# Six-layer kernel on one core: the RWKV layer's reciprocal as exp(-ln x), its norms and last product on other engines

## What is computed

```python
x = _layernorm(x, ln_g, ln_b)
last_x = jnp.pad(x[:, :-1], ((0, 0), (1, 0), (0, 0)))
k = (x * time_mix_k + last_x * (1.0 - time_mix_k)) @ Wk.T     # v and r likewise
td = jnp.exp(time_decay)
def step(carry, kv):                                          # over the tokens
    num, den = carry; kt, vt = kv                             # kt = exp(k)
    den = den * td + kt
    num = num * td + kt * vt
    return ((num, den), num / (den + 1e-08))
out = jax.nn.sigmoid(r) * wkv @ Wo.T
```

## Time and profile before

| | us |
|---|---|
| median of 3 runs | 2185.0 |
| lowest, highest | 2184.05, 2187.51 |
| profiled execution, its own time | 2186.31 |
| span of that execution | 2184.6 |
| TensorE busy in the span | 1656.4 (76%) |
| VectorE busy | 1514.8 (69%) |
| ScalarE busy | 965.0 (44%) |
| GpSimd busy | 1043.2 (48%) |

### The profile page before, as it was taken

How to read it: one execution, slowest core, us unless ns; L and a number is a source line. 1 busy time by engine, 2 the same in 40 slices (tenths; PEclk the granted TensorE clock), 3 DMA queues, 4 the chain that set the end, 5 groups by cost and what they waited for, 6 DMA issues and landing times.

```text
span 2184.6 us, 43737 instructions
## 1 busy us (share of the span) xinstructions
PE 1656.4 (76%) x11008; PEld 1493.4 (68%) x11008; DVE 1514.8 (69%) x4465; ACT 965.0 (44%) x2292; POOL 1043.2 (48%) x1639
## 2 busy tenths in 40 slices
PE   6499999378838999985168996269999974199993
PEld 6399999366627999984157776268888863177772
DVE  6678888288876888886546665758888865366664
ACT  2476665022207666632035554036666621055551
POOL 3537675378832455324633333605666625533331
PEclk9999999599969999985589998559999965599996
DMA  3110000720001001020111111202111101111115
GB/s 154 35 35 31 30 30 2 186 52 0 0 7 54 31 25 29 16 80 31 39 50 50 51 39 43 58 22 69 58 58 56 49 1 41 51 47 51 47 35 159
DMA packets 95511, 103.82 MB, mean 48 GB/s; under 512 B 12328, under 2 KB 75965, under 8 KB 94880
## 3 DMA queue, kind: packets, MB, share of 16 engines
q1 hardware_dynamic: 62144, 72.42, 10.7%
q10 hardware_dynamic: 23328, 12.67, 2.5%
q0 software_dynamic: 9920, 17.35, 2.4%
HBM read 67.94 MB, written 37.97 MB: 48 GB/s over the span
## 4 chain that ended last, share of the span: by engine, by line
PE 40%; DVE 30%; issue 14%; ACT 5%; another core or an unknown queue 2%; POOL 2%; DMA 2%; DVEq 2%; ACTq 1%; SPq 1%; POOLq 0%
PE banks L533 5%; ACT top_hhi L592 3%; PE banks L1037 3%; DVE bnstats L238 3%; DVE rwkv_over L1516 3%; PE banks L522 2%; PE banks L1024 2%; PE banks L1039 2%; PE banks L1038 2%; PE banks L1026 2%; PE banks L1025 2%; DVE top_hlo L752 2%; PE banks L1060 2%; PE banks L1059 2%
## 5 line engine op out<-in xcount | busy, mean ns | idle before, releaser
L803 POOL DMA_INDIRECT rt_y<-top_y,top_xs x182 | 178.8, 982 | 331.4 <-DVE top_y L760 307.8
L1235 DVE TENSOR_TENSOR choice_hlo<-choice_h,choice_hhi 128x512 fp32r<-128x512 f32 x256 | 180.1, 744 | 89.7 <-ACT choice_hhi L1122 89.5
L1114 ACT ACTIVATE choice_h<-banks 128x512 f32<-128x512 f32 x256 | 152.4, 599 | 160.7 <-PE banks L1026 142.5
L752 DVE TENSOR_TENSOR top_hlo<-banks,top_hhi 128x384 fp32r<-128x384 f32 x182 | 101.4, 557 | 144.6 <-ACT top_hhi L592 130.4
L796 POOL DMA_INDIRECT rt_rows<-top_payload,top_slot x128 | 129.7, 1013 | 131.2 <-DVE top_slot L713 94.0
L533 PE MATMUL banks<-t_w,top_hhi 128*128 x364 | 131.0, 360 | 45.9 <-DVE top_hlo L752 23.1
L746 DVE SCALAR_TENSOR_TENSOR top_h<-top_silu,top_xs,banks 128x176 f32<-128x176 f32 x364 | 128.4, 394 | 45.7 <-ACT top_silu L587 43.6
L1037 PE MATMUL banks<-choice_hhi,ec_w_hi 128*128 128x256 f32 x512 | 147.6, 288 | 4.2 <-DVE choice_hlo L1235 3.5
L1024 PE MATMUL banks<-choice_xin_hi,ec_w_hi 128*128 128x256 f32 x512 | 147.2, 287 | 4.7 <-ACT choice_xin_lo L1107 4.7
L1122 ACT ACTIVATE choice_hhi<-choice_h 128x512 fp32r<-128x512 f32 x256 | 146.4, 624 | 0.0
L1026 PE MATMUL banks<-choice_xin_hi,ec_w_lo 128*128 128x256 f32 x512 | 143.8, 281 | 0.0
(11 more groups left out here) (305 smaller groups left out, 5835.5 us busy)
## 6 DMA issues: line engine op xcount, KB each, us to landing
choice_token_row<-choice_tokens SPq DMA_DIRECT2D x64, 256.0 KB, 3.1
mlstm_run_row<-mlstm_run SPq DMA_DIRECT2D x32, 512.0 KB, 3.6
rt_rows<-rt_blank ACTq DMA_DIRECT2D x2, 6188.0 KB, 35.4
top_xs<-rt_rows SPq DMA_DIRECT2D x182, 68.0 KB
top_y_in<-rt_y SPq DMA_DIRECT2D x16, 512.0 KB, 7.2
X<-in_x SPq DMA_DIRECT2D x8, 512.0 KB, 6.8
ec_stage<-in_ec_w SPq DMA_DIRECT2D x2, 2048.0 KB, 15.6
out_x<-X SPq DMA_DIRECT2D x8, 512.0 KB, 7.6
```

Source lines behind the costliest of these rows:

```text
L803: pool.indirect_dma_start(d.y[self.run], bass.IndirectOffsetOnAxis(ap=at, axis=0), self.y[:, u % self.YR, :], None, bounds_check=NT * P - ...
L1114: act.activation(self.h[:, c, :], self.ph[c][:, :], ACT.Gelu).then_inc(self.gelu_done, 1)
L1235: dve.tensor_tensor(flat(self.hlo), self.h[:, c, :], flat(self.hhi).bitcast(F32), ALU.subtract).then_inc(self.hlo_done, 1)
```

## The change

What it does, in the RWKV layer:

- VectorE's reciprocal is replaced. ScalarE makes log = ln(under) and guess = exp(-log); VectorE makes off = under * guess and over = (off - 2) * guess, one Newton step, which gives minus the reciprocal; the sign is taken back by a negated copy of Wo, made once. er1 is capped at 1e18.
- The product z = num * over goes from VectorE to GpSimd.
- This layer's norm and the next layer's norm go from GpSimd (two passes) to ScalarE, as Identity with a scale and a bias per partition, one instruction for each 128 tokens. The bias, -mean/std, is one more small GpSimd product per sequence, in this layer's and in the layer before's scale step.
- Output and update of a sequence come one step later, and the statistics, scale, next layer's transposes, copies and scores too; there is one more step in the pipeline. The loop is entered after eight steps in place of six. Next layer's norm stays at its place (s-4 on ScalarE, where it was s-3 on GpSimd).

```diff
@@ Moments
-            self.chains.append(Chain(steps, self.PER[kind == "rwkv"], base))
+            per = 7 if kind == "rwkv" else 2 if self.by_scalar(n) else 1
+            self.chains.append(Chain(steps, per, base))
...
+        def product(ins):
+            ch.link(pool, ins)
+            return pool.tensor_tensor(flat(self.nmrs), flat(self.nm), flat(self.rs), ALU.mult)
@@ Normed
+    def scalar(self, act, b, u, xn_free):
+        m = self.sh.moments
+        act.wait_ge(m.scaled, self.layer * B + b - self.o + 1)
+        xn_free()
+        for t in range(TP):
+            scale, bias = (v[:, bass.ds(b - self.o, 1), t:t + 1].rearrange("p a t -> p (a t)") for v in (m.rs, m.nmrs))
+            i = act.activation(self.xn[:, u, t, :], self.sh.X[:, bass.ds(TP * (b - self.o) + t, 1), :].rearrange("p a c -> p (a c)"),
+                               ACT.Identity, scale=scale, bias=bias)
+        i.then_inc(self.done, 1)
@@ Rwkv.tensor
-            if self.next is not None and inside(b - 6):
-                pe.wait_ge(self.next.xT_done, self.next.o + b - 5)
+            if self.next is not None and inside(b - 7):
+                pe.wait_ge(self.next.xT_done, self.next.o + b - 6)
...
-            if inside(s - 1):
-                out(s - 1, 1 - u)
+            if inside(s - 2):
+                out(s - 2, u)
...
-                if inside(s + 1) and inside(s - 4):
+                if inside(s + 1) and inside(s - 5):
                     pe.wait_ge(self.x1_done, s + 2)
-                self.ahead_for_next(pe, self.next.turn_first, s - 4, u)
-                self.ahead_for_next(pe, self.next.score, s - 5, 1 - u)
+                self.ahead_for_next(pe, self.next.turn_first, s - 5, 1 - u)
+                self.ahead_for_next(pe, self.next.score, s - 6, u)
@@ Rwkv.scalar
+        def guess(b, u):
+
+            act.wait_ge(self.under_done, b + 1)
+            need(act, self.over_done, 2 * (b - 1))
+            act.activation(self.log[:, u, :], self.under[:, u, :], ACT.Ln).then_inc(self.guess_done, 1)
+            act.wait_ge(self.guess_done, 2 * b + 1)
+            act.activation(self.guess[:, u, :], self.log[:, u, :], ACT.Exp, scale=-1.0).then_inc(self.guess_done, 1)
...
         def step(s, u):
+            if inside(s - 1):
+                guess(s - 1, 1 - u)
             if inside(s + 1):
                 x1(s + 1, 1 - u)
             if inside(s):
                 exps(s, u)
+            if inside(s + 2):
+                norm(s + 2, u)
             if self.next is not None:
-                self.ahead_for_next(act, self.next.first_xT, s - 4, u)
+                self.ahead_for_next(act, self.next.first_norm, s - 4, u)
+                self.ahead_for_next(act, self.next.first_xT, s - 5, 1 - u)
 
         self.sh.start(act, self.x0)
+        norm(0, 0)
+        norm(1, 1)
         act.wait_ge(self.w_in, 32)
@@ Rwkv.vector
-            dve.reciprocal(self.over[:, u, :], self.under[:, u, :]).then_inc(self.over_done, 1)
-            dve.wait_ge(self.over_done, b + 1)
-            need(dve, self.out_done, b - 1)
-            dve.tensor_tensor(self.z[:, u, :], self.num[:, u, :], self.over[:, u, :], ALU.mult).then_inc(self.z_done, 1)
+        def improve(b, u):
+
+            dve.wait_ge(self.guess_done, 2 * b + 2)
+            dve.tensor_tensor(self.off[:, u, :], self.under[:, u, :], self.guess[:, u, :], ALU.mult).then_inc(self.over_done, 1)
+            dve.wait_ge(self.over_done, 2 * b + 1)
+            if not isinstance(b, int) or b >= 2:
+                apart(dve, self.z_done, b - 1, sh.passed)
+            dve.scalar_tensor_tensor(out=self.over[:, u, :], in0=self.off[:, u, :], scalar=-2.0, in1=self.guess[:, u, :],
+                                     op0=ALU.add, op1=ALU.mult).then_inc(self.over_done, 1)
...
         def step(s, u):
-            self.moments_next(dve, s - 2, u)
             if inside(s):
                 mix(s, u)
+            self.moments_next(dve, s - 3, 1 - u)
             if inside(s - 1):
-                update(s - 1, 1 - u)
+                improve(s - 1, 1 - u)
+            if inside(s - 2):
+                update(s - 2, u)
...
+        dve.tensor_scalar(self.wo[:, :], self.w[:, 3, :], -1.0, None, ALU.mult).then_inc(self.setup, 1)
@@ Rwkv.gpsimd
+        def product(b, u):
+
+            apart(pool, self.over_done, 2 * b + 2, self.sh.passed)
+            if not isinstance(b, int) or b >= 2:
+                apart(pool, self.out_done, b - 1, self.sh.passed)
+            pool.tensor_tensor(self.z[:, u, :], self.num[:, u, :], self.over[:, u, :], ALU.mult).then_inc(self.z_done, 1)
 
         def step(s, u):
-            if inside(s + 2):
-                norm(s + 2, u)
             if inside(s):
                 er1(s, u)
-            self.scale_next(pool, s - 2, u)
-            if self.next is not None:
-                self.ahead_for_next(pool, self.next.first_norm, s - 3, 1 - u)
+            self.scale_next(pool, s - 3, 1 - u)
+            if inside(s - 1):
+                product(s - 1, 1 - u)
```

More of the change, by code:

```diff
@@ L42 @@
 ROUND = float(1 << 23)
+FAR = 1.0e18
 FB = 4
@@ L198, in __init__ @@
         self.rs = mem.take("rstd", [P, B, TP])
+        self.nmrs = mem.take("negmean_rstd", [P, B, TP])
         self.stats, self.moments, self.scaled = sh.sem("stats_done"), sh.sem("moments_done"), sh.sem("scaled")
@@ L202, in __init__, with by_scalar @@
         for n, kind in enumerate(LAYERS):
-            self.chains.append(Chain(steps, self.PER[kind == "rwkv"], base))
-            base += (B if n else XC) * self.PER[kind == "rwkv"]
-    PER = (1, 6)
+            per = 7 if kind == "rwkv" else 2 if self.by_scalar(n) else 1
+            self.chains.append(Chain(steps, per, base))
+            base += (B if n else XC) * per
+    def by_scalar(self, layer):
+        return "rwkv" in LAYERS[max(layer - 1, 0):layer + 1]
     def moments_of(self, dve, layer, b, u):
@@ L255, in rstd @@
         ch.link(pool, pool.tensor_scalar(sm[:, 0, :], var, 1.0, EPS_LN, ALU.mult, ALU.add))
-        if ch.per > 1:
+        def product(ins):
+            ch.link(pool, ins)
+            return pool.tensor_tensor(flat(self.nmrs), flat(self.nm), flat(self.rs), ALU.mult)
+        if ch.per > 2:
             ch.link(pool, pool.tensor_tensor(sm[:, 1, :], sm[:, 0, :], half, ALU.pow))
@@ L262, in rstd @@
             ch.link(pool, pool.tensor_tensor(sm[:, 3, :], sm[:, 2, :], half, ALU.pow))
-            i = pool.tensor_tensor(flat(self.rs), sm[:, 1, :], sm[:, 3, :], ALU.mult)
+            i = product(pool.tensor_tensor(flat(self.rs), sm[:, 1, :], sm[:, 3, :], ALU.mult))
         else:
             i = pool.tensor_tensor(flat(self.rs), sm[:, 0, :], half, ALU.pow)
+            if ch.per > 1:
+                i = product(i)
         ch.end()
@@ L960, in pfirst, with first_norm @@
         return self.sh.banks[7][:, T:2 * T] if self.ahead else self.sh.banks[u][:, 0:T]
-    def first_norm(self, pool, b, u):
-        self.norm.gpsimd(pool, b, u, lambda: apart(pool, self.xT_ready, b - 1, self.sh.passed), self.o)
+    def first_norm(self, act, b, u):
+        self.norm.scalar(act, b, u, lambda: need(act, self.xT_ready, b - 1))
     def turn_first(self, pe, b, u):
@@ L1390, in __init__ @@
         self.x1 = f("x1", [P, 2, T + 1])
-        self.ek, self.er, self.er1, self.ekv, self.num, self.den, self.under, self.over, self.z = (
-            f(n, [P, 2, T]) for n in ("ek", "er", "er1", "ekv", "num", "den", "under", "over", "z"))
+        self.ek, self.er, self.er1, self.ekv, self.num, self.den, self.under, self.z = (
+            f(n, [P, 2, T]) for n in ("ek", "er", "er1", "ekv", "num", "den", "under", "z"))
+        self.log, self.guess, self.off, self.over = (f(n, [P, 2, T]) for n in ("log_under", "guess", "guess_off", "over"))
+        self.wo = f("w_out_negative", [P, C])
         bk = sh.banks
@@ L1434, in project @@
             need(pe, self.ekv_done, b - 1)
-            need(pe, self.er_done, b - 1)
+            need(pe, self.exps_done, 2 * (b - 1))
             for n, (o, done) in enumerate(((self.pkv[u][:, 0:T], None), (self.pkv[u][:, T:2 * T], self.kv_done),
@@ L1479, in exps, with norm @@
             need(act, self.scans_done, b - 1)
-            act.activation(self.ek[:, u, :], self.pkv[u][:, 0:T], ACT.Exp).then_inc(self.ek_done, 1)
+            act.activation(self.ek[:, u, :], self.pkv[u][:, 0:T], ACT.Exp).then_inc(self.exps_done, 1)
             act.wait_ge(self.r_done, b + 1)
             need(act, self.er1_done, b - 1)
-            act.activation(self.er[:, u, :], self.pr[u][:, 0:T], ACT.Exp, scale=-1.0).then_inc(self.er_done, 1)
+            act.activation(self.er[:, u, :], self.pr[u][:, 0:T], ACT.Exp, scale=-1.0).then_inc(self.exps_done, 1)
+        def guess(b, u):
[4 more added lines that the diff above has]
+            act.activation(self.guess[:, u, :], self.log[:, u, :], ACT.Exp, scale=-1.0).then_inc(self.guess_done, 1)
+        def norm(b, u):
+            self.norm.scalar(act, b, u, lambda: need(act, self.xT_ready, b - 1))
```

(2 more changed lines are left out.)

24 lines of the change are left out of this document (11 added, 13 removed).

## The result

The changed kernel takes 2212.2 us (median of 4) against 2186.1 before: a ratio of 1.0123, 95% interval 1.011 to 1.0135. Slower, as forecast, by twice as much: +26 us, where the sum said +13.

The account below looks back on a forecast made before the run. The prediction took VectorE to bound the RWKV layer before, and ScalarE with two table loads after: four intervals at 5.3 us and 27 at 6.4 give +12.2, start +1.6, end -0.7, so 2199 us, range 2184 to 2226.

Parts of the forecast that it names:

- the sum: Whole program: RWKV layer +12.2 us, start +1.6, end -0.7, in all +13.1 on 2186.3 us, giving 2199.
- no wait, and both loads are exposed: ScalarE's ln: `under` ready at about 6.3 us, ln not before 7.47, so neither table load hides in a wait.
- the clock's term: TensorE at 1.2 GHz delays er by 0.73 us in one step of 3.5, 0.2 us a step.
- Two loads a step: ScalarE in the RWKV layer: ln and the next Exp each load their own set, 2.60 us a step.
- One load for all: ScalarE's ln brings a set that keeps Exp; 5.7 us a step, 2176 us, faster; chance 0.10.
- The fourth rival: ScalarE's table loads cost more, a drain of 1.38 us each by the skill's page: 2278 or 2285 us; chance 0.02.
- ScalarE's chain: ScalarE's queue over one RWKV step, from xT copy's end to the next with two loads: 6.17 us.
- The second rival: Idle TensorE draws more steps at the lower clock: 6.9 us a step, 2212 us; chance 0.14.
- er1 0.4: GpSimd's er1 in each RWKV step counted as 0.4 us, within some 4.2 us of GpSimd work.
- Rows 7: Profile rows of ScalarE's table loads: 1.28 us each, one 1.35 us ahead of its Exp, not waiting for data.
- The ends: Before and after the layer's steady steps: start +1.6 us for norms on ScalarE, end -0.7 us from last `under` to softmax.
- The third rival's ring: GpSimd's scale and z, small instructions stretched beside VectorE: 0.8 us more per round, 2210 us; chance 0.10.

Follow-up runs that it names:

- e2: Changed kernel with one table load, of the set holding Exp and Ln, placed by hand ahead of the decay's exp: 1.0031 of the kernel before.
- e4: Changed kernel with one hand-placed table load and er1 as before, without the cap: 0.9960 of the kernel before.
- e12: Changed kernel with ScalarE's wait for the Newton step made earlier, so the table load precedes the wait for `under` in both loop steps: 1.0085 of the kernel before.
- e13: Changed kernel with the table load ahead of the wait for `under` in both loop steps and er1 as before: 1.0094 of the kernel before.
- e6: Changed kernel without the three matmuls per sequence that project the token before: 1.0066 of the kernel before.
- e10: Changed kernel without the three matmuls projecting the token before, and with er1 as before: 1.0059 of the kernel before.
- e7: Changed kernel with one table load, er1 as before, and the next layer's transposes and copy ahead of output matmuls and norms: 0.9924 of the kernel before.
- e14: Kernel of e7 with the product z back on VectorE behind the Newton step: 0.9867 of the kernel before.
- e9: Kernel of e7 with GpSimd's product z ahead of the scale step in its queue: 1.0052 of the kernel before.
- e1_er1: Changed kernel with er1 = er * 1 + 1 as before, in place of min(er + 1, 1e18): 1.0100 of the kernel before.
- e3_busy_pe: Changed kernel with four unused transposes of the identity on TensorE at the end of each step: 1.0125 of the kernel before.
- after: The changed kernel as first measured, unedited: 2212.2 us, 1.0123 of the kernel before.

## Why the prediction was half right

The direction, its main cause and three of the prediction's signs came true: 64 loads, ScalarE busy 93%, VectorE waiting 1.9 us a step for ek. The size was half of what was measured. The step that failed is the sentence "no wait, and both loads are exposed": one of the prediction's own signs of being wrong, ln waiting for `under`, showed in every second step. Beside it the clock's term was too small.

**Two loads a step: right.** 64 loads of 1.283 us, each exposed, and e2 takes them out for 20 us. The ground given (a load is chosen by the one function that lacks) is borne out as far as a trace can: with a load of the common set ahead none is placed.

**One load for all: wrong as it stood, right as a remedy.** e2 and e4 show the common set at work. The fourth rival, a drain behind each load, is refuted: ln and the guess's exp start 1.29 us after their loads, as the time order shows.

**ScalarE's chain: right.** 6.17 forecast, 6.25 measured in e12 and e13. Activations that read SBUF took 0.417 instead of 0.383, the scaled copies 0.485 instead of 0.46.

**The clock: right in kind, too small.** The sum took 0.73 us in one step of 3.5, 0.23 a step with what was rounded up: 27 x 0.23 = 6.2 us. Measured: 8.2 by e6 against the changed kernel; 7.1 and 7.4 by what e12 and e13 have over 6.25 a step, in which slow steps are rarer and cost 0.88 and 0.82. What the sum had wrong for the changed kernel is the count, about 8 slow steps where it has one in two. The second rival had that count, and its time, 2212, is the measured one. That is luck: it has all of the missing time as clock, and e12 shows that a good part was the load's place.

**er1: a term that failed.** The prediction wrote "er1 0.4", the row of the kernel before. The change writes another pair of operations and, by shortening VectorE's side, puts it beside the scans: 1.45 us. With this `under` was ready not 6.3 but 7.0 to 7.4 us after the copy's end (525.89 - 518.88, and in the slow step behind it 532.91 - 525.50). By itself that costs nothing: ln could not start before 7.47 by the sum, and e12, with the long er1, has its steps at 6.25. It counts where a load waits for `under`: 0.48 us in e6, 0.28 in e10 with er1 as before.

**"No wait, and both loads are exposed": the step that failed.** In one of two steps the load wasn't ahead of the wait for `under`, so that wait came on top of both loads, and `under` came later than I had it. Rows 7 were read as if a load always goes ahead; they show one that does. Together these two cost 4.3 us by the waits ahead of the loads, 5.8 by what e6 has over 6.25 a step, and 203.6 - 196.5 = 7.1 by e12, where slow steps also became rarer. They and the clock act on each other, so no sharper split is shown.

**The sum again, for the `under` span.** Forecast 192.5, measured 203.6, 11.1 more. Over 6.25 us a step the changed kernel has 14.1 us, which is 5.8 for the load's place with er1 and 8.2 for the clock by e6, or 7.1 and 7.1 by e12. The sum had 6.2, for the clock alone: 7.9 more. Some 2.2 are ScalarE's 0.08 us a step; about 1 us is left without a name.

**The ends.** Start: the first `under` comes 3.0 us later, where 1.6 was the sum; 1.1 of it is the layer before, whose end moved as much (ScalarE's first norm at 423.12 where the load stood at 422.01), so 1.9: the norms' 1.65 and a part of er1's longer time. End: from the last `under` to the softmax 14.8 us against 13.3 (640.0 to 654.8), +1.5 where the sum had -0.7. The last z starts 5.9 us behind the last `under` (640.0 to 645.9) where it was 2.2; most of that comes back behind it, but not all. From the softmax to the program's end the profiled execution is 2.0 us shorter than before, which the sum had at nothing; runs of one kernel differ by as much.

**GpSimd's ring: right in e7, not in the changed kernel.** The third rival's ring (scale, z) isn't what held the steps at 6.83 (e12 has 6.25 with GpSimd's work unchanged), but it is what holds e7 at 5.4, and e14 takes it out.

## What to carry over

A new table function costs what its set costs: before two functions alternate in a loop, ask which set each would load when asked for alone, and place one load of the common set by hand. An operation that keeps its place in the code but gets other operands, another op pair or another neighbour is a new operation and has to be costed as one. And when a queue is reordered, ask not only who waits for what moves up, but what then stands behind its wait (e9).

## What the runs showed of the hardware

- GpSimd's tensor_scalar of 128x256 took 0.40 us as (mult, add) and 1.11 us as (add, min), without a neighbour; beside VectorE's scans 0.79 and 1.45 (e1_er1, e3_busy_pe, after).
- An activation of 128x256 took 0.417 us from SBUF (ln and the guess's exp) and 0.37 to 0.38 from PSUM (ek and er); a 128x128 one with scale and bias per partition 0.48 to 0.50.
- A table load took 1.283 us each of 64 times, and the next activation started 0.01 us behind it in the steady steps.
- TensorE's clock fell to 1.2 GHz for 3.4 us (512.0 to 515.4) in every second step of the changed kernel, and 0.63 us a step of idle transposes changed its mean from 0.88 to 0.87, at a busy share of 73% and 80%. In e7_copy_first and, from 500 to 560 us, in e14_z_on_vector it stayed at 2.4 GHz (mean 1.00), with a busy share of 77% and 90%. So the mean busy share of a stretch didn't tell the clock here.
